# Scores for the maxima before scores by keys within each tick of a two-layer attention kernel

## The reference, cut to what matters

```python
scores = jnp.einsum('bhqd,bhkd->bhqk', q, k) / np.sqrt(HD)       # layer 0; keys after the query are masked
attn = jnp.einsum('bhqk,bhkd->bhqd', softmax(scores), v)         # out_w, a residual, 8 steps of a recurrence, a GELU feed-forward
...
result = jnp.einsum('bsd,od->bso', x, weight) + pooled @ disha   # a linear layer and a norm
...
attn = jnp.einsum('bhqk,bkhd->bqhd', softmax(scores), v)         # layer 1; no mask; then a ReLU feed-forward and a norm
```

## Time and profile before

| | us |
|---|---|
| median of 3 runs | 1529.98 |
| lowest and highest | 1524.67, 1530.46 |
| profiled execution, its time | 1526.45 |
| profiled execution, its span | 1524.7 |
| PE, DVE, ACT, POOL busy in the span | 1369.9, 1249.3, 1081.6, 278.1 |
| body of the attention of layer 0, about | 75 to 480 |
| body of the attention of layer 1, about | 780 to 1420 |

### The profile page before, as it was taken

How to read it: one execution, slowest core, us unless ns; L and a number is a source line. 1 busy time by engine, 2 the same in 40 slices (tenths; PEclk the granted TensorE clock), 3 DMA queues, 4 the chain that set the end, 5 groups by cost and what they waited for, 6 DMA issues and landing times.

```text
span 1524.7 us, 31977 instructions
## 1 busy us (share of the span) xinstructions
PE 1369.9 (90%) x13016; PEld 565.3 (37%) x13016; DVE 1249.3 (82%) x1715; ACT 1081.6 (71%) x1239; POOL 278.1 (18%) x624
## 2 busy tenths in 40 slices
PE   6699999999998768888679999999999999999886
PEld 3333434343343334446423333233333333233355
DVE  7978888888885387885989999999999999997143
ACT  6167777777777657764358888888888888887642
POOL 4021322223133132332200000000000000001252
PEclk9689999999999899999889999999999999999998
DMA  5610110101100000012120000000000000000001
GB/s 177 168 45 24 31 38 25 45 24 42 27 4 3 1 1 0 1 65 82 42 64 23 23 24 23 14 17 18 23 23 23 23 23 23 3 3 3 1 15 42
DMA packets 38995, 47.90 MB, mean 31 GB/s; under 512 B 11072, under 2 KB 20160, under 8 KB 38720
## 3 DMA queue, kind: packets, MB, share of 16 engines
q1 hardware_dynamic: 38416, 45.31, 10.1%
q10 hardware_dynamic: 432, 0.53, 0.1%
HBM read 30.22 MB, written 15.47 MB: 30 GB/s over the span
## 4 chain that ended last, share of the span: by engine, by line
PE 62%; DVE 23%; ACT 6%; issue 4%; POOL 3%; SPq 1%; DMA 1%; POOLq 0%; ACTq 0%; DVEq 0%
PE ps L426 22%; DVE l_negp L324 14%; PE ps L404 12%; PE ps L383 12%; PE ps L552 7%; ACT shared L296 3%; PE ps L443 2%; PE ps L389 2%; POOL n_rs L514 2%; DVE n_bst L495 2%; PE ps L545 1%; PE ps L1040 1%; SPq L113 1%; PE ps L908 1%; PE ps L560 1%
## 5 line engine op out<-in xcount | busy, mean ns | idle before, releaser
L324 DVE TENSOR_REDUCE l_negp<-ps 128x2 f32<-128x1024 f32 (+2 forms) x832 | 953.3, 1181 | 75.5 <-PE ps L389 36.4
L296 ACT ACTIVATE shared<-ps 128x1024 f32<-128x1024 f32 (+1 forms) x832 | 820.4, 991 | 196.8 <-PE ps L404 168.1
L426 PE MATMUL ps<-shared,l_vs 128*32 128x256 f32 (+3 forms) x6648 | 515.3, 386 | 4.1 <-POOL shared L280 3.3
L383 PE MATMUL ps<-Ks,Qs 48*128 48x512 bf16 (+3 forms) x1792 | 329.9, 369 | 40.6 <-DVE l_negp L324 27.2
L404 PE MATMUL ps<-Qs,Ks 51*128 51x512 bf16 (+3 forms) x1792 | 320.8, 366 | 25.5 <-ACT shared L296 10.7
L404 PEld LDWEIGHTS ps<-Qs,Ks 51*128 51x128 bf16 x1792 | 81.3, 93 | 330.6 <-issue 159.3
L426 PEld LDWEIGHTS ps<-shared,l_vs 128*32 128x32 f32 x6648 | 134.8, 108 | 172.3 <-issue 141.7
L383 PEld LDWEIGHTS ps<-Ks,Qs 48*128 48x128 bf16 x1792 | 87.6, 94 | 194.3 <-ACT shared L296 91.0
L280 POOL TENSOR_SCALAR_AFFINE_SELECT shared<-shared 128x512 f32<-128x512 f32 x128 | 81.7, 639 | 321.0 <-ACT shared L296 320.9
L265 POOL CAST l_parts<-l_negm 128x16 bf16<-128x16 f32 x64 | 12.6, 197 | 441.8 <-DVE l_negm L329 438.6
L389 PE MATMUL ps<-mask,id 64*128 64x128 bf16 x1024 | 69.2, 223 | 0.0
(11 more groups left out here) (160 smaller groups left out, 1090.4 us busy)
## 6 DMA issues: line engine op xcount, KB each, us to landing
Qs<-scr_q SPq DMA_DIRECT2D x128, 64.0 KB
Ks<-scr_k SPq DMA_DIRECT2D x64, 96.0 KB
Qs<-scr_q SPq DMA_DIRECT2D x128, 32.0 KB
Ks<-scr_k SPq DMA_DIRECT2D x64, 64.0 KB
scr_q<-own SPq DMA_DIRECT2D x4, 768.0 KB, 3.6
scr_q<-shared SPq DMA_DIRECT2D x4, 768.0 KB, 3.5
scr_k<-own SPq DMA_DIRECT2D x4, 768.0 KB, 5.0
scr_k<-shared SPq DMA_DIRECT2D x4, 768.0 KB, 4.8
```

What stands on the lines that cost most here:

```text
L296: act.activation(dst, src, ACT.Exp, scale=SCALE).then_inc(exped, 1)
L324: dve.tensor_reduce(dst, src, AX_X, ALU.max, negate=True).then_inc(reduced, 1)
L383: last = pe.matmul(outs[par], Qs[s][r:r + MROW, h2, qt * P:(qt + 1) * P], Ks[s][r:r + MROW, h2, at:at + w], start=True, stop=True)
L426: last = pe.matmul(pv_ps[q % 2][32 * h:32 * h + 32, a:a + wide], vs[g % 2][:, kt, h, :], pT[m % PRING][:, h, a:a + wide], start=m == u.fir ...
```

## The change

One pair of names changes place in the table that orders the entries of one tick. Each tick's max unit now stands ahead of its key unit.

```diff
-        kinds = ("split", "key", "max", "weigh", "evacuate", "turn_max", "turn_out")
+        kinds = ("split", "max", "key", "weigh", "evacuate", "turn_max", "turn_out")
```

## The result

| | before | with the change |
|---|---|---|
| median (runs) | 1528.76 us (4) | 1609.57 us (4) |
| lowest and highest | 1524.67, 1530.46 | 1607.38, 1610.72 |
| span of the profiled execution | 1524.7 | 1607.9 |

The ratio is 1.053, with a 95% interval of 1.0507 to 1.0553: 81 us slower. The prediction said 1602, in a range of 1565 to 1620.

A forecast was written before the change was run, and what follows sets the result against it. A closed loop through PE and the exponential, 2.40 us for two ticks, was taken as the bound. The profiled 1526.45 + 47 (layer 1) + 27 (layer 0) = 1600, stated as 1602 us, range 1565 to 1620.

The forecast's parts named there:

- The loop K, W, M, reduction: Key unit, weigh, next max unit, its reduction, back to key unit: 2.60 us for two ticks, 1.30 a tick against 1.20.
- DVE's rival: Both layers: DVE, 96.5% busy in layer 1, is the bound, so no change, 1530 us; chance 0.05.
- Layer 1: Halves of layer 1 walked through: 1.55 us more each, 30.4 halves, +47 us; bounds +27 to +58.
- the turns cost what they cost: At the turns of layer 1's halves: their cost stays as before, so a half gains 16 x 0.10 = 1.6 us.
- Layer 0: Groups of 20 ticks: 28.6 us against 26.77, +1.8 for 14.8 groups, +27 us; bounds +9 to +36.
- Rival D: Layer bodies: PE's clock falls as PE waits in each tick, 70 us on top, 1672 us; chance 0.04.
- granted clock 1.00 in both bodies: Expected sign in the changed profile: PE keeps its full clock in the bodies of layers 0 and 1.
- the bounds 1562 to 1624: Whole kernel: lowest and highest time in us from the bounds of both layers' slowdowns, around 1602.
- A: Both layers: the new loop over the reduction slows the kernel to 1602 us, anything from +35 to +95; chance 0.84.
- B: Both layers: DVE's own pace is the bound, so both orders cost the same, 1530 us; chance 0.05.
- C: Both layers: key unit's wait for DVE isn't felt, DVE's 1.14 a tick sets the pace, 47 us less, 1483; chance 0.05.
- the rest: Whole kernel: a slowdown below +35 us; chance 0.02.

The follow-up runs named there:

- the short readers: Layer 1's reductions over half the keys, or exponentials over half the queries: kernel before 1516.10 and 1500.87 us, changed kernel 1508.03 and 1603.49.
- short exponentials: Each exponential of layer 1 over half its unit's queries: 1500.87 us on the kernel before, 1603.49 us on the changed kernel.
- one tick of lead: Kernel before with each max unit, split and turn_max one tick earlier (`longest + 11` for `+ 10`): 1511.98 us, ratio 0.9871.

## Why the prediction was right

**The mechanism.** The loop K, W, M, reduction was forecast at 2.60 for two ticks and is 2.61, each of its pieces within 0.01. It is shown three ways: by the trace after; by the short readers, which move the halves much only where they are in the loop; and by the row with key first and weigh between (2.61) against the row with max first and weigh behind it (2.40).

**What DVE's rival missed.** DVE was 96.5% busy before, yet with short exponentials its reductions came 1.13 apart and the halves at 19.48. That DVE sets the pace held at most around the turns: shorter reductions took 0.21 off a half of the kernel before.

**Layer 1.** Forecast +47 (1.55 a half), measured +48.7, from the last exponential (1437.5 before, 1520.4 after) and the loading of its table that opens layer 1 (779.9 and 814.1), and +50 with the change in layer 1 alone. Halves are 21.95, 0.15 longer than walked through and 0.12 more than the sum took, which makes 30.4 x 0.12 = 3.6 us. That the turns cost what they cost was right: 21.95 - 16 x 1.305 = 1.07, against 1.08 before.

**Layer 0.** A group was walked through at 28.6 and takes 28.55. With the change in layer 0 alone the time is +29, where the forecast said +27. One term was missing: three groups have a stretch at the half clock, 1.5 us each.

Up to the start of layer 1 the changed profile is 34.2 us behind, 7 more than forecast. That isn't the change. At the last division of layer 0 it is 27.5 behind (522.14 and 549.64), and the other 6.7 come in the stage between the layers, whose order is the same. Its clock and busy times, before, with the change, and with the change in layer 1 alone, where the list up to there is that of the kernel before:

```profile
522.00:780.00 258.00, 197.55 (x880) 116.90 (x879) 199.24 (x418) 143.72 (x175) 67.64 (x103) 0.94 0.11 36
```

```profile
550.00:814.00 264.00, 205.87 (x881) 121.95 (x879) 199.81 (x418) 143.69 (x174) 67.12 (x102) 0.89 0.10 36
```

```profile
516.88:781.58 264.70, 206.40 (x881) 122.07 (x880) 200.25 (x419) 143.80 (x174) 67.54 (x103) 0.89 0.11 36
```

With layer 0 in the order of before, this stage takes 257.8, 264.7 and 264.2 us (kernel before, layer 1 alone, short exponentials), and with the change 264.5, 260.7 and 263.8 (change, layer 0 alone, short exponentials). It differs by 7 us between profiles in either order, at a mean clock of 0.94 in the shortest and 0.89 in the longest.

**Rival D** was given 0.04 as a whole and was true in part. I had weighed the clock by the mean busy share of the bodies (91% forecast); it fell behind a place where 0.79 of 1.40 us were idle. The step that failed is "granted clock 1.00 in both bodies": three times 1.5 us. With the 3.6 of layer 1 that is about the 8 us by which 1602 was short. In layer 1 no such place exists and the clock is 1.00 throughout.

**Slips in the working.** Of the bounds 1562 to 1624 the lower stands on the profiled execution and the upper on the median; on one base they are 1562 to 1620. And the chances leave more outside 1565 to 1620 than 2 in 10: a fifth of A's 0.84 is 0.17, and B, C, D and the rest are 0.16, together a third.

**Open:** why key, weigh, max is milder in layer 0, what decides whether the clock falls behind the idle place, and which meeting of units gives the 0.9 us a group that one tick of lead brings.

## What to carry to other kernels

Where entries of two kinds share a ring of buffers, write down for each wait the closed loop that it makes: the reader, its latency on both sides, and everything that stands in the issuing engine's list between the released matmul and the one that feeds the reader again. Where the longest such loop divided by its ticks is longer than the busiest engine's own row, the loop sets the pace; here it explained 2.40 and forecast 2.60, which came out at 2.61. Long work should stand in the loop of the faster reader, and it is the cyclic row that counts, not who is first in a tick; what is placed once a half (a turn, an evacuation) has to be followed through each new row by itself.

## What the runs showed of the hardware

- Weigh of two heads (four instructions with 32 output rows) takes 0.56 us, nearly the same as weigh of four heads (eight instructions, 0.57).
- The clock fell to its half for about 3.6 us behind a place with PE busy 0.61 of 1.40 us (220.00 to 221.40), in three groups of layer 0. The same place of the next group (250.05 to 251.45, also 0.61 of 1.40) was followed by the full clock.
- A matmul of weigh starts 0.32 behind a key or max unit, a key or max unit 0.23 behind the other kind, and 0.57 behind weigh. Either cyclic order of the three has one of each, 1.12 a tick; with the change and short reductions it was 1.11.
- Reductions whose data is ready start 1.13 apart, though each is recorded at 1.22: eleven took 12.54 us.
